# The quantised feed-forward of a two-layer decoder as one unrolled stream

## The reference

```python
def act_qdq(x):
    scale = max(max(abs(x)) / 32767, 1e-12)
    return clip(round(x / scale), -32768, 32767) * scale

def fixed_qdq_u16(x):
    return clip(round(x * 65536), 0, 65535) / 65536

x = layernorm(x5)                      # 4096 x 256, then:
x = act_qdq(x)
up = act_qdq(x @ W_up.T)               # 4096 x 768
gate = act_qdq(x @ W_gate.T)           # 4096 x 768
sig = fixed_qdq_u16(sigmoid(gate))
gate = act_qdq(gate * sig)
o = act_qdq(gate * up)
out = x5 + o @ W_down.T                # 4096 x 256
```

## Time and profile before

| | |
|---|---|
| median of 3 runs | 1876.58 us |
| the profiled execution's own time | 1876.91 us |
| its span (first to last instruction) | 1875.3 us |
| TensorE matmul busy | 1555.1 us (83%) |
| VectorE busy | 986.9 us (53%) |
| ScalarE busy | 871.9 us (46%) |
| GpSimd busy | 435.4 us (23%) |
| mean granted TensorE clock | 0.92 of full speed |
| first instruction of the feed-forward | 1458.26 us from the span's start |

### The profile page before, as it was taken

How to read it: one execution, slowest core, us unless ns; L and a number is a source line. 1 busy time by engine, 2 the same in 40 slices (tenths; PEclk the granted TensorE clock), 3 DMA queues, 4 the chain that set the end, 5 groups by cost and what they waited for, 6 DMA issues and landing times. The chain is left out here.

```text
span 1875.3 us, 27409 instructions
## 1 busy us (share of the span) xinstructions
PE 1555.1 (83%) x10044; PEld 1078.4 (58%) x10044; DVE 986.9 (53%) x2215; ACT 871.9 (46%) x1820; POOL 435.4 (23%) x563
## 2 busy tenths in 40 slices
PE   4999999999875499999959999999996699740189
PEld 2666766676653287877736666666665343310177
DVE  3565657766655252222135565656453336888822
ACT  2346565555453122121126565556663337877611
POOL 3123233434333200000056444543331000000000
PEclk9999999999987699999979999999997799875599
DMA  3340111101311434343431111110000000000112
GB/s 103 125 150 19 42 32 45 39 30 42 105 35 49 144 104 149 109 144 120 116 107 42 31 43 33 50 38 1 16 15 23 0 0 1 0 0 0 46 66 68
DMA packets 99630, 107.08 MB, mean 57 GB/s; under 512 B 25266, under 2 KB 88508, under 8 KB 99504
## 3 DMA queue, kind: packets, MB, share of 16 engines
q1 hardware_dynamic: 93360, 88.83, 15.2%
q0 software_dynamic: 6144, 16.57, 2.7%
HBM read 63.59 MB, written 42.01 MB: 56 GB/s over the span
## 5 line engine op out<-in xcount | busy, mean ns | idle before, releaser
L1866 ACT ACTIVATE c_pr<-bank,c_nmax 128x256 f32<-128x256 f32 x256 | 118.1, 475 | 151.0 <-DVE c_nmax L1947 150.9
L2417 PE MATMUL bank<-wdT,hT_all 128*128 128x256 f32 x384 | 89.1, 397 | 119.5 <-DVE hT_all L2395 119.5
L1619 POOL TENSOR_SCALAR c_pr<-c_pr,c_rsum 128x256 f32<-128x256 f32 x256 | 128.7, 518 | 223.1 <-DVE c_rsum L1952 223.0
L1386 ACT ACTIVATE b_G<-bank 128x320 f32<-128x320 f32 x128 | 56.0, 437 | 209.5 <-PE bank L1336 209.5
L1336 PE MATMUL bank<-b_XT,shared 128*128 128x320 f32 x512 | 153.3, 434 | 0.0
L2417 PEld LDWEIGHTS bank<-wdT,hT_all 128*128 128x128 f32 x384 | 76.8, 201 | 132.2 <-DVE hT_all L2395 120.7
L1350 PE MATMUL bank<-shared,b_G 128*128 128x256 f32 x640 | 142.2, 379 | 0.0
L1350 PEld LDWEIGHTS bank<-shared,b_G 128*128 128x128 f32 x640 | 120.9, 190 | 17.8
L947 DVE TENSOR_TENSOR a_A<-bank,a_causal 128x512 f32<-128x512 f32 x128 | 79.4, 683 | 73.8 <-PE bank L475 73.7
L1947 DVE TENSOR_REDUCE c_nmax<-bank 128x2 f32<-128x512 f32 x128 | 82.2, 683 | 55.0 <-PE bank L1658 54.9
L1336 PEld LDWEIGHTS bank<-b_XT,shared 128*128 128x128 f32 x512 | 91.7, 191 | 27.0 <-issue 0.2
(11 more groups left out here) (287 smaller groups left out, 3403.5 us busy)
## 6 DMA issues: line engine op xcount, KB each, us to landing
shared<-L_ffn_w SPq DMA_DIRECT2D x32, 512.0 KB, 6.0
t_slots_in<-a_h SPq DMA_DIRECT2D x20, 512.0 KB, 6.7
shared<-t_slots_in SPq DMA_DIRECT2D x15, 640.0 KB, 6.9
t_slots_out<-b_Y SPq DMA_DIRECT2D x15, 640.0 KB, 4.1
a_xin<-x SPq DMA_DIRECT2D x8, 512.0 KB, 3.7
a_xr<-x SPq DMA_DIRECT2D x8, 512.0 KB, 3.7
t_x_a<-hT_all SPq DMA_DIRECT2D x8, 512.0 KB, 2.9
shared<-t_x_a SPq DMA_DIRECT2D x8, 512.0 KB, 4.1
```

The costliest lines, as they stand in the source:

```text
L1386: a.activation(G[e % 2][:, f, HC * m:HC * m + HC], P[2 + n % 2][:, 0:HC], ACT.Gelu).then_inc(q.g_ready, 1)
L1619: p.tensor_scalar(pr[k][:, e, u, :], pr[k][:, e, u, :], rsum[k][:, e, u:u + 1], 1.0, ALU.mult, ALU.mult).then_inc(q.pr_ready, 1)
L1866: a.activation(pr[t % 2][:, e, u, :], P[e][:, S * u:S * u + S], ACT.Exp, bias=nmax[t % 2][:, e, u:u + 1], accum_out=sums[t % 2][:, e, u:u ...
L2417: t = p.matmul(P[n % 8][:, 0:D], tl[f"of{k % 2}"][:, f, 128 * j:128 * j + 128], wdT[:, f, :], start=(f == 0), stop=(f == FC - 1))
```

## The change

`layer1`: behind its loop GpSimd runs one more `partition_all_reduce`, of a tile that nobody needs, into another that nobody reads any more.

`feed_forward` is one block with no loop and no barrier inside; every wait is a semaphore between two engines.

- Tiles of gate and up are now 2 units wide (1024 columns), 24 of them.
- VectorE alone quantises the input, group by group (2 x 512 columns), two groups ahead of the gate's units.
- TensorE goes from the gate's last unit straight on to up's first.
- The sigmoid goes into one tile `sig`. GpSimd makes the 16-bit integers of every tile from it (two buffers `sq`). VectorE writes their product with the integer gate over the raw gate (`tile(n)` of `raw`), so the product stage reads it and doesn't make sigmoid and integers again.
- Up's raw values go into a buffer `up` of 13 tiles and into columns of `hT` that are no longer used; those of tiles 19, 20, 22 and 23 stay in PSUM.
- Product stage: ScalarE makes up's integers and a's integers, VectorE multiplies and takes the magnitude. Down is one stream of 32 results; the last four are stored one by one (128 KB).

```diff
@@ layer1, gpsimd
+                p.partition_all_reduce(rstd[0][:, 0:1], minus[:, 0:1], 128, RMAX).then_inc(q.c_pool, 1)
@@ feed_forward
-        with ExitStack() as once:
-            q = signals(...)
-            with nc.Fori(0, NG // K) as i:
-                with nc.Block() as block:
...
+        with nc.Block() as block:
+            @block.gpsimd
+            def _(p):
...
+                all_max("x", 0)
+                all_max("g", 1)
+                for n in range(NTILE):
+                    p.wait_ge(q.sig_ready, n + 1)
+                    if n >= 2:
+                        p.wait_ge(q.act_ready, n - 1)
+                    p.tensor_scalar(sq[n % 2], sig, 65536.0, 1.0, ALU.mult, ALU.mult).then_inc(q.sq_ready, 1)
+                all_max("u", 2)
+                all_max("a", 3)
+                all_max("o", 4)
+            @block.tensor
...
+                for m in range(NU):
+                    if m % FC == 0:
+                        p.wait_ge(q.xq_ready, m // FC + 1)
+                    if m >= 8:
+                        p.wait_ge(q.bank_free, m - 7)
+                    product(wgT, m, P[m % 8])
+                for m in range(NU):
+                    p.wait_ge(q.bank_free, NU + m - (7 if m < NU - 2 else 3))
+                    product(wuT, m, unit_bank(m))
...
+            @block.scalar
...
+                def gate_int(n):
+                    if n >= 3:
+                        a.wait_ge(q.act_ready, n - 2)
+                    a.activation(pair(gi[n % 3]), tile(n), ACT.Copy, scale=inv["g"][:, :]).then_inc(q.gi_ready, 1)
+                def sigmoid(n):
+                    if n:
+                        a.wait_ge(q.sq_ready, n)
+                    a.wait_ge(q.gi_ready, n + 1)
+                    a.activation(sig, gi[n % 3], ACT.Sigmoid, scale=scale["g"][:, :]).then_inc(q.sig_ready, 1)
...
+                for m in range(4):
+                    keep_up(m)
+                a.wait_ge(q.scaled, 2)
+                gate_int(0)
+                gate_int(1)
+                sigmoid(0)
+                for n in range(1, NTILE):
+                    if n + 1 < NTILE:
+                        keep_up(2 * n + 2)
+                    sigmoid(n)
+                    if n + 1 < NTILE:
+                        gate_int(n + 1)
+                    if n + 1 < NTILE:
+                        keep_up(2 * n + 3)
+                a.wait_ge(q.scaled, 3)
+                for n in range(NTILE):
+                    if n >= NI:
+                        a.wait_ge(q.prod_ready, n - NI + 1)
...
+                        x = a.activation(pair(u_room[n % NI]), up_tile(n), ACT.Copy, scale=inv["u"][:, :])
+                    x.then_inc(q.ui_ready, 1)
+                    if n:
...
+                        a.activation(pair(a_room[n % NI]), tile(n), ACT.Copy, scale=inv["a"][:, :]).then_inc(q.ai_ready, 1)
...
+            @block.vector
...
+                def activate(n):
+                    v.wait_ge(q.gi_ready, n + 1)
+                    v.wait_ge(q.sq_ready, n + 1)
+                    v.tensor_tensor(tile(n), pair(sq[n % 2]), pair(gi[n % 3]), ALU.mult).then_inc(q.act_ready, 1)
...
+                make_scale("x", 0)
+                quantise_input(0)
+                quantise_input(1)
+                for m in range(NU):
+                    gate_magnitude(m)
+                    if m % FC == 1 and m // FC + 2 < NG:
+                        quantise_input(m // FC + 2)
...
+                for m in range(4):
+                    up_magnitude(m)
+                for n in range(NTILE):
+                    activate(n)
+                    if n + 2 < NTILE:
+                        up_magnitude(2 * n + 4)
+                    if n + 1 < NTILE:
+                        act_magnitude(n)
+                    if n + 2 < NTILE:
+                        up_magnitude(2 * n + 5)
+                v.wait_ge(q.bank_free, 2 * NU)
+                largest("u")
+                act_magnitude(NTILE - 1)
+                largest("a")
+                make_scale("u", 2)
+                make_scale("a", 3, (scale["g"][:, :], 1.0 / 65536.0))
+                v.tensor_scalar(pair(a_room[0]), tile(0), inv["a"][:, :], None, ALU.mult).then_inc(q.ai_first, 1)
+                for n in range(NTILE):
+                    product(n)
+                    if n:
+                        product_magnitude(n - 1)
+                product_magnitude(NTILE - 1)
```

More of the change, by code:

```diff
@@ L2179, in feed_forward @@
-        TP = T // 2
-        NPC = 8
-        def carve(tiles, width):
-            room = c.hT_all[:, :, :].rearrange("p c t -> p (c t)")
-            at, out = 0, {}
-            for k, dt in tiles:
-                words = FC * width // (1 if dt == F32 else 2)
-                part = room[:, at:at + words]
-                out[k] = (part if dt == F32 else part.bitcast(dt)).rearrange("p (f t) -> p f t", f=FC)
-                at += words
-            assert at <= 2 * B * S
-            return out
@@ L2207, in products @@
-        def products(p, i, wT, cur_ready, r_psum):
-            for n in range(K * FC):
-                k, f = n // FC, n % FC
-                if n >= 8:
-                    p.wait_ge(cur_ready, n - 7)
-                for u in range(2):
-                    t = p.matmul(P[n % 8][:, :], wT[:, u, 128 * f:128 * f + 128], c.hT_all[:, u, bass.ts(K * i + k, T)],
-                                 start=(u == 0), stop=(u == 1))
-                t.then_inc(r_psum, 1)
-        def keep_product(a, i, n, r_psum, raw_ready):
-            a.wait_ge(r_psum, n + 1)
-            a.activation(raw[:, n % FC, bass.ts(K * i + n // FC, T)], P[n % 8][:, :], ACT.Copy).then_inc(raw_ready, 1)
@@ L2222, in feed_forward @@
-        make_scales(("x", c.amax, None, None))
-        quantise_input()
-        with ExitStack() as once:
-            q = signals(nc, once, "g_psum_d graw_ready gcur_ready gcur_total gcur_done")
-            with nc.Fori(0, NG // K) as i:
-                with nc.Block() as block:
-                    @block.vector
-                    def _(v):
-                        for n in range(K * FC):
-                            bank_magnitude(v, n, q.graw_ready, q.gcur_ready)
-                        running(v, cur, K * FC, q.gcur_ready, mx, q.gcur_total, q.gcur_done)
-                    @block.tensor
-                    def _(p):
-                        products(p, i, wgT, q.gcur_ready, q.g_psum_d)
-                    @block.scalar
-                    def _(a):
-                        for n in range(K * FC):
-                            keep_product(a, i, n, q.g_psum_d, q.graw_ready)
-                clear(nc, q)
@@ new lines, in feed_forward @@
+        NOWN = 13
+        up = sb("up", [128, NOWN * W])
+        cur = {k: sb("cur_" + k, [128, n]) for k, n in (("g", NU), ("u", NU), ("a", NTILE), ("o", NTILE))}
+        top = {k: sb("top_" + k, [128, 1]) for k in "guao"}
+        top["x"] = c.amax
+        gmx = {k: sb("gmx_" + k, [128, 1]) for k in "xguao"}
+        scale = {k: sb("scale_" + k, [128, 1]) for k in "xguao"}
+        inv = {k: sb("inv_" + k, [128, 1]) for k in "xguao"}
+        unit = {k: sb("unit_" + k, [128, 1]) for k in "ao"}
@@ new lines, in feed_forward, with pair @@
+        spare = wgT[:, :, :].rearrange("p c n -> p (c n)")
+        sig = spare[:, 0:W]
+        sq = [spare[:, W:W + T].bitcast(U16), sb("sig_int", [128, W], U16)[:, :]]
+        gi = [sb(f"gate_int_{k}", [128, W], I16)[:, :] for k in range(3)]
+        NI = 3
+        a_room = gi
+        u_room = [sig.bitcast(I16)[:, W * k:W * k + W] for k in range(2)] + [sq[1].bitcast(I16)]
+        def pair(ap):
+            return ap.rearrange("p (f t) -> p f t", t=T)
+        IN_BANKS = (19, 20, 22, 23)
@@ new lines, in unit_bank, with up_tile, tile, kept_until @@
+        def unit_bank(m):
+            return P[m % 8] if m < NU - 2 else P[m % 8 - 4]
+        def up_tile(n):
+            if n < NOWN:
+                return pair(up[:, W * n:W * n + W])
+            i = n - NOWN if n < 19 else NG - 2
+            return hT[:, :, T * i:T * i + T]
+        def tile(n):
+            f = n % (FC // 2)
+            g = n // (FC // 2)
+            return raw[:, 2 * f:2 * f + 2, T * g:T * g + T]
+        def kept_until(m):
+            return NU + sum(k // 2 not in IN_BANKS for k in range(m + 1))
@@ new lines, in feed_forward @@
+        of = [pair(up[:, NG * NT * D:NG * NT * D + FC * T]), pair(hT[:, 0, 0:FC * T])]
+        oi = [pair(hT[:, 1, FC * T // 2 * k:FC * T // 2 * k + FC * T // 2].bitcast(I16)) for k in range(2)]
+        xin = [up[:, NT * D * g:NT * D * g + NT * D].rearrange("p (j n) -> p j n", j=NT) for g in range(NG)]
+        PIECES = [(0, 0, T // 2), (0, T // 2, T // 2)] + [(g, 0, T) for g in range(1, NG)]
+        x_rows = dr["x_c"].rearrange("(i j p) n -> i p j n", p=128, j=NT)
+        out_rows = out.rearrange("(i j p) n -> i p j n", p=128, j=NT)
@@ L2423 @@
+        clear(nc, q)
 class Common:
```

352 lines of the change are left out of this document (134 added, 218 removed).

## The result

The changed kernel took 1797.17 us (median of 4 runs, 1791.86 to 1800.33), the kernel before 1876.83 in the same comparison: a ratio of 0.9567, with a 95% interval of 0.9534 to 0.9600. The prediction said 1791.5 in a range of 1785 to 1806. A repeat gave 1795.58 and 0.9573. The profiled execution is the 1791.86 one, the fastest of its four, with a span of 1790.1 us against 1789.9 predicted.

What follows compares the result with a forecast made beforehand. Bound taken as TensorE's pace (gate, down), VectorE's pace (up with activation, product) and seams; the change attacks the last two. Stage ends 1542.6, 1640.0, 1695.2, 1785.7 plus a 4.2 tail gave span 1789.9, time 1791.5 us; range 1785 to 1806.

Steps and rivals of the forecast that it cites:

- the sigmoid's integers off VectorE: Up with activation: GpSimd converts in 1.12 us a tile, taking only 6 us off VectorE; VectorE sets 3.46 us a tile.
- The product stage: Product: one VectorE pass in three removed and no round in the middle; 55 us instead of 93.5, 38 us gained.
- the entry: Layer 1's end to first gate matmul: code load beside the tail, TensorE starts at 1457.0 not 1468.2, 11 us gained.
- gate: Gate projection: TensorE alone sets the pace, 85.6 us after its first matmul, ending at 1542.6.
- turn: From gate's end to the first activation: ScalarE copies, integer tiles, table load, sigmoid and GpSimd's conversion, 13.2 us.
- T: The predicted end of gate, 1542.6, from which the activation steps were counted.
- down: Down projection: one stream of 32 results at 2.59 us plus 3.3, 86.2 us, from 1699.5 to 1785.7.
- tail: TensorE's last matmul to the span's end: 4.2 us, bounds 3 and 4.5, with 128 KB in place of 512 KB.
- Loose steps: Rival: semaphores between four engines leave VectorE bubbles of 0.2 to 0.5 us on 24 tiles, +5 to +12; chance 0.17.
- Blocking: Rival: GpSimd conversions and two-input VectorE instructions exclude each other, at worst 27 us; chance of over 10 us 0.09.
- GpSimd as the bound: Rival: uint16 conversions slower than 2.2 us a tile lengthen every tile; at 7 us, 115 us more; chance 0.02.
- The clock: Rival: TensorE gets the 1.2 GHz level for half its 168 us stream, stages growing by 80 us; chance 0.02.

Runs made afterwards that it cites:

- magnitude_twice: Changed kernel with VectorE taking the magnitude of every product tile twice: 1833.89 us, ratio 0.9712 to the kernel before.
- dve_converts: Changed kernel with VectorE instead of GpSimd making the sigmoid's 16-bit integers for every tile: 1812.0 us, ratio 0.9652 to the kernel before.
- down_seam: Changed kernel with only the seam in the middle of the down projection put back: 1818.43 us, ratio 0.963 to the kernel before.
- no_preload: Changed kernel without the extra all-reduce at the end of layer 1: 1794.77 us, ratio 0.955 to the kernel before.
- root_by_scalar: Changed kernel with layer 1's last normalisation taking its root from ScalarE and reciprocal from VectorE, not GpSimd's power: 1785.74 us, ratio 0.9509 to the kernel before.
- early_start: Changed kernel with ScalarE making the first scaled gate tiles between its copies of up, not behind four of them: 1800.52 us, ratio 0.9552 to the kernel before.
- combined_root: Changed kernel with root_by_scalar, early_start and 32 useless TensorE matmuls ahead of down together: 1785.77 us, ratio 0.9511 to the kernel before.
- combined_short: As combined_root, with 22 useless matmuls in place of 32: 1781.08 us, ratio 0.9505 to the kernel before.
- x_by_tensor: Changed kernel with x's maximum over partitions found by TensorE and VectorE, and layer 1's extra all-reduce removed: 1794.55 us, ratio 0.9544 to the kernel before.

## Why the prediction was right, and where it was not

**Right in kind.** Three mechanisms were named. A VectorE pass less in the product stage is shown by magnitude_twice (26.8 us), the sigmoid's integers off VectorE by dve_converts (14.3), the seam in the middle of down by down_seam (8.8). The other seams (11 us in the product stage, 8.3 in gate, those in up) and the quantisation by groups are read from the two traces and were not put back one by one. The product stage was the largest term, and it came out as the sum had it: 55.7 us from a's scale to the last magnitude, 55.2 predicted.

**The step that failed: the entry.** I wrote that the load starts beside layer 1's tail, the real all-reduce near 1454.7 and TensorE at 1457.0, and "if the load can't overlap the tail, 4 us come back". From the last power (1444.98 before, 1444.14 after) I had allowed 12.0 us to the first gate matmul; it took 16.3. The load does overlap the tail; but GpSimd's drain of 5.3 us can't begin before it and closes the block. I had put all of GpSimd's unexplained 12.26 us down to loading (7.3) and layer 1's own tail. no_preload shows the preload's worth (nothing), root_by_scalar the drain's (8.0 us with the load). The loading itself is 5.5 to 6.1 us where the trace says "issue" before an all-reduce, and 6.9 to 7.1 back to the scaling code in early_start and the two combined kernels. The Trainium skill, "GPSIMD Engine Reference", section 2.1, puts it at about 6 us, and the rows of the all-reduce agree; my 7.3, from the kernel's first instruction, was too long, and had I asked what else the 12.26 us held once 6 were taken off, the drain was there to be found.

**Small terms, with opposite signs.** Against the predicted steps: layer 1 ended 0.8 us sooner; entry +4.3; gate 84.3 us to its last copy for 85.6, -1.3; turn as predicted (13.3 for 13.2); activation to a's scale 96.7 for 97.4 after T, -0.7; product and the steps behind it +0.6; down 85.4 for 86.2, -0.8; tail 3.2 for 4.2, -1.0. Together +0.3. So the span's 0.2 us of error is the sum of a miss of 4.3 and several that hide it. The median lies 5.7 us above 1791.5 for a reason that the prediction had left out: the whole program's scatter, of which the two profiled executions happened to show the same end of layer 1 (last `c_var_eps` at 1444.7 and 1443.9); most later profiles had it at 1447 to 1463. Only one profile of the kernel before was taken, so whether its layer 1 ends as late as often isn't shown, and with it why the medians lie 79.7 us apart and not 84 or 85.

**The rivals.** *Loose steps:* false. Behind the first tiles the period was 3.46 us, and the act column is 80.5 in every kernel that left the stage alone. *Blocking:* real, and harmless. At the first tiles, before the rhythm is found, conversions lasted 1.39 and 1.80 us instead of 1.04 and one multiply 2.04 instead of 1.21: 0.8 us of VectorE lost once. The timeline of that place:

```profile
1564.97 1.22 DVE L2339 TENSOR_TENSOR d_raw<-wgT,d_gate_int 128x1024 f32<-128x1024 uint16 x1
1565.29 1.80 POOL L2199 TENSOR_SCALAR d_sig_int<-wgT 128x1024 uint16<-128x1024 f32 x1 [1.66 <-ACT wgT L2250]
1568.35 1.04 POOL L2199 TENSOR_SCALAR wgT<-wgT 128x1024 uint16<-128x1024 f32 x1 [1.26 <-ACT wgT L2250]
1568.43 2.04 DVE L2339 TENSOR_TENSOR d_raw<-d_sig_int,d_gate_int 128x1024 f32<-128x1024 uint16 x1
```

Each time the one that started later, 0.3 or 0.1 us into the other, was stretched by nearly all that the other still needed. That is the rule of the Trainium skill, "SBUF — State Buffer", section "Who interferes with whom"; the rows agree with it. After that the wait on `act_ready` places every conversion of this kernel behind a multiply, under magnitudes, and nothing is lost, not even at twice the conversions. The wait does not force it: in early_start twelve conversions ran into a multiply (1.91 to 2.17 us), and the period held because it has room, the 2.2 us a tile of the forecast. *GpSimd as the bound:* false at 1.04 us, and at two conversions a tile; but where it does bite first is not the period: it is the code load behind the last conversion. *The clock:* 0.98 over the gate and 0.95 over the up stretch, with no fall in the long stream.

**What stays open.** Why GpSimd's drain takes 5.3 us at the end of layer 1 (and of layer 0, 5.29) but some 0.1 in the feed-forward's block. The two slow ones close blocks in which GpSimd issued indirect DMAs; no run took those away. Nor was it tried to load GpSimd's code less often within the feed-forward, which now sets the first activation.

## What to carry to other kernels

When an engine's unexplained idle time stands before a barrier, look at that engine's closing drain as well as at code loading: a preload put ahead of a drain buys nothing, while moving the engine's last small instruction elsewhere bought 8 us here. A free engine that is slower at a job (1.04 us for 0.72) still wins if each period leaves room for the job at its longest (2.17 us here, when it ran into the other engine's instruction); measure its margin at the end of the stream too, not only within it. And on one core, whose runs scatter by several us, compare stage by stage from a common event in the profiles: columns that should not move then show how far one can trust those that do.

## What the runs showed of the hardware

- GpSimd's drain at the end of a block ended 5.3 us after its last instruction in each of the fourteen profiles, wherever that instruction stood.
- Changing GpSimd from its scaling code to the all-reduce cost 5.5 to 6.1 us, and back again 6.9 to 7.1 where nothing hid it (early_start, combined_root, combined_short), although both had run before.
- GpSimd turned 1024 float32 columns into uint16 in 1.043 us; VectorE in 0.68.
- A conversion of GpSimd that started 0.04 us into a VectorE multiply of two SBUF tensors took 2.07 us instead of 1.04, and the multiply its usual 1.21; a multiply that started 0.1 us into a conversion took 2.04.
- TensorE's first 5 us of gate or down, after a pause of 4.25 us (root_by_scalar) or longer (in x_by_tensor two tiny matmuls lie in it), had a granted clock of 0.50 (the 1.2 GHz level throughout) to 0.68, and 1.00 (2.4 GHz) when matmuls of no use went before, also across a pause of 0.84 us.
- A table load on ScalarE ran ahead of the wait of the instruction that it was for (1431.85, the root at 1438.76), and so cost nothing.
